# Hops of a four-layer graph network in blocks of 64 tiles, with the scalar chain in two independent halves

## The reference

```python
head_emb = entity_emb[head]; tail_emb = entity_emb[tail]
rel_emb = relation_emb[relation_type]
ricci = _l2_normalize(tail_emb + rel_emb)
hyper_head = expmap0(head_emb)                 # tanh(n) * u / n
hyper_tail = expmap(tail_emb, hyper_head)      # mobius_add(p, tanh(...) * u / n)
hyper_rel = expmap(rel_emb, hyper_head)
res = project(mobius_add(hyper_tail, hyper_rel))
res = jax.nn.relu(logmap(res, hyper_head) + ricci * 1e-07)
sums = zeros.at[head].add(res)                 # then / clip(counts, 1)
...
for _ in range(2):
    e = _l2_normalize(_agg(e, relation_emb, head, tail, relation_type))
    entity_res_emb = 0.5 * entity_res_emb + e
```

## Time and profile before

| | |
|---|---|
| median of three runs | 23802.61 us |
| profiled execution | 24039.33 us |
| its span, mean granted TensorE clock | 24037.5 us, 0.618 |
| DVE busy | 16546.3 us, 69% |
| POOL busy | 12605.7 us, 52% |
| PE busy, weight loads | 10326.4 us, 43%; 6860.3 us, 29% |
| ACT busy | 2139.0 us, 9% |
| hop 0, hop 1 in the span | 16471 to 20166, 20277 to 23976 us |
| DVE busy in each | 2929.34 us, 2935.75 us |

### The profile page before, as it was taken

One profiled execution on the slowest core, in us unless ns is written; L12 is line 12 of the kernel. 1 busy time (PEld: TensorE's weight loads), 2 busy tenths in 40 slices (PEclk: granted clock), 3 DMA queues, 4 the chain that ended last, 5 costly groups with the idle time before them and its releaser, 6 DMA issues. The chain is left out here.

```text
span 24037.5 us, 205919 instructions
## 1 busy us (share of the span) xinstructions
PE 10326.4 (43%) x47565; PEld 6860.3 (29%) x47566; DVE 16546.3 (69%) x26071; ACT 2139.0 (9%) x3670; POOL 12605.7 (52%) x12782
## 2 busy tenths in 40 slices
PE   0033326655555555556666422222333333333333
PEld 0033322222222222222222322222333332333332
DVE  8744439988888888886666211115888886878887
ACT  0011110000000000000000000001111111111111
POOL 0188876655566555536665166653444443444443
PEclk9999997555555555558887555555555555555555
DMA  4133331111111111121112001113111112111112
GB/s 170 25 69 69 69 64 25 24 23 23 22 21 23 23 23 23 22 20 24 24 24 23 9 21 21 21 21 49 52 51 50 51 50 41 52 51 50 52 50 42
DMA packets 1118452, 942.42 MB, mean 39 GB/s; under 512 B 775931, under 2 KB 887579, under 8 KB 1117875
## 3 DMA queue, kind: packets, MB, share of 16 engines
q0 software_dynamic: 419904, 437.84, 9.9%
q1 hardware_dynamic: 698096, 500.67, 8.0%
HBM read 726.46 MB, written 207.32 MB: 39 GB/s over the span
## 5 line engine op out<-in xcount | busy, mean ns | idle before, releaser
L1420 POOL DMA_INDIRECT tail<-ball,h_idx x3328 | 3271.7, 983 | 1793.3 <-issue 1231.1
L736 PE MATMUL p_rad<-w_stack,hid_t 99*128 99x512 bf16 (+1 forms) x6656 | 3079.6, 620 | 2391.3 <-DVEq L826 1161.0
L808 DVE TENSOR_REDUCE red<-prod 128x96 f32<-128x1536 f32 x1664 | 2898.3, 1742 | 3.5
L1098 POOL DMA_INDIRECT l_xg<-h_tab,l_idx x1664 | 1571.2, 944 | 1444.1 <-issue 828.3
L1452 PE MATMUL h_sum<-head,h_hot 128*128 128x64 f32 x6656 | 1444.2, 421 | 1987.4 <-ACT head L1498 1987.4
L1438 PE MATMUL h_head<-ball_parts,hot_t 128*128 x9984 | 1067.6, 281 | 2813.4 <-issue 1578.1
L337 POOL DMA_INDIRECT rec_a<-rec,slot x1600 | 1990.4, 1244 | 517.2 <-issue 500.5
L692 POOL DMA_INDIRECT rec_b<-l_rcb x1600 | 1920.0, 1200 | 571.6 <-issue 570.5
L930 POOL DMA_INDIRECT l_xg<-x_tab,l_idx x1664 | 1571.6, 944 | 1141.8 <-issue 874.0
L946 PE MATMUL l_sum<-outer,l_hot 128*128 128x512 f32 x3328 | 1693.3, 673 | 945.6 <-DVEq L991 869.7
L736 PEld LDWEIGHTS p_rad<-w_stack,hid_t 99*128 99x128 bf16 (+1 forms) x6656 | 774.5, 132 | 4337.7 <-issue 4336.0
(11 more groups left out here) (369 smaller groups left out, 18896.7 us busy)
## 6 DMA issues: line engine op xcount, KB each, us to landing
hot_t<-rows_l SPq DMA_DIRECT2D x208, 512.0 KB
rec_a<-fill SPq DMA_DIRECT2D x128, 728.0 KB, 19.6
l_rec<-rec_a SPq DMA_DIRECT2D x104, 896.0 KB, 4.8
rhot_t<-rows_r SPq DMA_DIRECT2D x208, 384.0 KB
tail<-ball,h_idx POOLq DMA_INDIRECT x3328
t<-in_type SPq DMA_DIRECT2D x100, 500.0 KB
l_xg<-in_x,l_idx POOLq DMA_INDIRECT x1664
l_xg<-x_tab,l_idx POOLq DMA_INDIRECT x1664
```

Source lines behind the costliest of these rows:

```text
L736: ins = pe.matmul(p_rad[j % 2][:, h * 512:(h + 1) * 512], hid_t[j // 4 % 2][0:K3 + 3 * (1 - i), j % 4, i, :], w_stack[i][0:K3 + 3 * (1 - i ...
L808: ch.step(dve.tensor_reduce(red[:, j, :], prod[j % 3][:, :, :], AX, ALU.add))
L1420: pool.indirect_dma_start(tg[q][:, j, :], None, table[:, :], bass.IndirectOffsetOnAxis(ap=idx[q][:, j:j + 1], axis=0)).then_inc(gathered[q ...
```

## The change

A block is HU = 4 units, 64 tiles, 26 blocks per hop. `op` issues each operation of the chain twice, for tiles 0 to 31 and 32 to 63, and each waits only for the last but one. Heads (`hg`), relations (`rg`), `tr` and PSUM's relation buffer have one copy instead of two; tails keep two. The hot matrices are made in half units (8 tiles) in two buffers, behind the products of each unit, and wait for the sums that last used the buffer. PE sums first, then picks b+1; its relation matmuls wait for the copies of the quad before. ACT does its four functions, four relus, then 16 quads in a row. POOL reads indices that SP loads per block from DRAM, waits after gathers 13, 26, 39, 52 and 64, and is let go unit by unit. DVE's compares of b+1 stand in the waits for tanh (two units) and behind the adds (two units); tails and heads of b+1 come last. The diff, cut:

```diff
+HU = 4
@@ hop_phase
-        W, Q, H = 2 * BT, BT // 2, BT // 4
+        W, Q, H, N2 = HU * BT, HU * BT // 4, BT // 4, HU * BT // 2
-        hot = sb("h_hot" + tag, [P, W, P])
+        hot = [sb(f"h_hot{k}" + tag, [P, HP8, P]) for k in range(2)]
-        hg = [sb(f"head{q}" + tag, [P, W, T_PICK]) for q in range(2)]
-        rg = [sb(f"rel{q}" + tag, [P, W, D + 2]) for q in range(2)]
+        hg = sb("head" + tag, [P, W, T_PICK])
+        rg = sb("rel" + tag, [P, W, D + 2])
-        p_rel = [ps(f"h_rel{k}" + tag, [P, 4, P]) for k in range(2)]
+        p_rel = ps("h_rel" + tag, [P, 4, P])
@@ sync
+            def body(b, q, it, left):
+                rows(b, 0)
+                rows(b, 1)
+                if left:
+                    hold(sp, turn, tails_read, b + 1)
+                    lists(b + 1, 1 - q)
+                    hold(sp, turn, ends_used, b + 1)
+                    edge_ends(b + 1, 1 - q)
+                rows(b, 2)
+                rows(b, 3)
@@ gpsimd
-                    hold(pool, turn, tails_used, b + 1)
-                    ch.do(pool.tensor_copy(idx[q][:, :], g["dst_b"][:, bass.ds(b * W, W)]))
+                    hold(pool, turn, idx_in[q], it * 16 + 16)
                     for j in range(W):
+                        if j % BT == 0:
+                            hold(pool, turn, tails_used, b * HU + (j // BT + 1))
...
-                        if j % 8 == 7:
+                        if j % 13 == 12 or j == W - 1:
                             hold(pool, turn, gathered[q], it * (16 * W) + 16 * (j + 1))
@@ tensor
+                    hold(pe, turn, taken, b * Q + (k + 2))
                     for j in range(4):
-                            ins = pe.matmul(p_rel[k % 2][:, j, 0:D + 2], rhot_t[h][:, 4 * i + j, :], rel_parts[:, :], start=True, stop=True)
+                        ins = pe.matmul(p_rel[:, j, 0:D + 2], rhot_t[u % 2][:, 4 * i + j, :], rel_parts[:, :], start=True, stop=True)
...
             def body(b, q, it, left):
-                if left:
-                    pick(b + 1)
                 hold(pe, turn, added, b + 1)
...
+                if left:
+                    pick(b + 1)
@@ vector
+            def hots(q, b, m):
+                z = slice(m * HP8, m * HP8 + HP8)
+                if m >= 2:
+                    dve.wait_ge(sum_done, b * (2 * HU) + (m - 1))
...
                 def op(f):
-                    z = slice(0, W)
+                    for half in range(2):
+                        z = slice(half * (W // 2), (half + 1) * (W // 2))
...
-                    ch.sync()
-                    ch.step(f(S, S2, E, B2, z))
+                        if ch.n > 1:
+                            dve.wait_ge(chain_s, ch.n - 1)
+                        ch.step(f(S, S2, E, B2, z))
...
-                hots(q, b, 0)
+                if left:
+                    compares(b + 1, 0)
+                    compares(b + 1, 1)
                 dve.wait_ge(told, b * 4 + 1)
...
-                hots(q, b, 1)
+                if left:
+                    relation_hots(1 - q, it + q)
                 dve.wait_ge(told, b * 4 + 2)
...
+                for u in range(HU):
+                    z = unit(u)
                     for vec, c in ((h, 16), (t, 18), (r, 19)):
                         ch.step(tt(vec[:, z, 0:D], vec[:, z, 0:D], bc(sc[:, c, z].unsqueeze(2), big), MUL_))
+                    load_chunks()
                     ch.sync()
-                    ch.do(tt(h[:, z, 0:D], h[:, z, 0:D], t[:, z, 0:D], ADD))
+                    ch.step(tt(h[:, z, 0:D], h[:, z, 0:D], t[:, z, 0:D], ADD))
+                    load_chunks()
+                    ch.sync()
+                    dve.sem_inc(tails_used, 1)
                     ch.do(tt(h[:, z, 0:D], h[:, z, 0:D], r[:, z, 0:D], ADD))
                     dve.sem_inc(asked, 1)
+                    for m in range(2):
+                        hots(q, b, 2 * u + m)
+                dve.sem_inc(ends_used, 1)
+                for u in range(HU):
+                    dve.wait_ge(sum_done, b * (2 * HU) + (2 * u + 2))
+                    add_groups(dve, ch, chunk[u * BG:u * BG + BG], acc, lambda k: p_sum[:, u * BG + k:u * BG + k + 1, :])
+                dve.sem_inc(added, 1)
                 if left:
+                    compares(b + 1, 2)
+                    tails(1 - q, it + q)
+                    compares(b + 1, 3)
+                    heads(1 - q, b + 1)
```

More of the change, by code:

```diff
@@ new lines, in quads @@
+            def quads(b):
+                for k in range(Q):
+                    hold(act, turn, picked, b * Q + (k + 1 + AHEAD))
+                    act.activation(hg[:, 4 * k:4 * k + 4, :], p_head[k % 2][:, :, 0:T_PICK], ACT.Copy).then_inc(copied, 1)
+                    act.activation(rg[:, 4 * k:4 * k + 4, :], p_rel[:, :, 0:D + 2], ACT.Copy).then_inc(copied, 1)
+                    act.wait_ge(copied, 2)
+                    act.sem_clear(copied)
+                    act.sem_inc(taken, 1)
@@ L1500, in _ @@
             act.activation(p_row[:, 0:P], g["row"][:, :], ACT.Copy).then_inc(row_ready, 1)
             act.sem_inc(taken, SEED)
-            for k in range(Q):
-                quad(0, 0, k)
+            quads(0)
             all_blocks(act, NW, body)
@@ new lines, in with_relation, with tails, heads @@
+            def with_relation(vec, out, u):
+                ch.do(tt(v2[:, :, 0:NREL3], vec[:, unit(u), T_REL:T_REL + NREL3], rhot[:, unit(u), :], MUL_))
+                ch.do(dve.tensor_reduce(out[:, unit(u)], v2[:, :, 0:NREL3], AX, ADD))
+            def tails(q, it):
+                dve.wait_ge(gathered[q], it * (16 * W) + 16 * W)
+                for u in range(HU):
+                    with_relation(tg[q], tr, u)
+                dve.sem_inc(tails_read, 1)
+            def heads(q, b):
+                t = tg[q]
+                for u in range(HU):
+                    z = unit(u)
+                    dve.wait_ge(taken, b * Q + ((u + 1) * H + SEED))
+                    with_relation(hg, sc[:, HV + 1, :], u)
+                    ch.do(tt(v2[:, :, :], hg[:, z, 0:D], t[:, z, 0:D], MUL_))
+                    ch.do(dve.tensor_reduce(sc[:, HV, z], v2[:, :, :], AX, ADD))
@@ L1700, in body, with load_chunks @@
                 big = [P, BT, D]
-                for half in range(2):
-                    z = slice(half * BT, half * BT + BT)
+                chunk = []
+                def load_chunks():
+                    chunk.extend(chunks(dve, g["map"][1], b * (N2 // PACK) + len(chunk) // PACK))
+                for u in range(HU):
+                    z = unit(u)
                     for vec, c in ((h, 16), (t, 18), (r, 19)):
                         ch.step(tt(vec[:, z, 0:D], vec[:, z, 0:D], bc(sc[:, c, z].unsqueeze(2), big), MUL_))
+                    load_chunks()
@@ L1715, in body @@
-                if left:
-                    tails(1 - q, b + 1, it + q)
-                    heads(1 - q, b + 1, load_chunks)
-                else:
-                    for _ in range(2 * BG // PACK):
-                        load_chunks()
-                if left == 2:
-                    compares(b + 2)
-                for half in range(2):
-                    dve.wait_ge(sum_done, b * 2 + (half + 1 + SEED))
-                    add_groups(dve, ch, chunk[half * BG:half * BG + BG], acc,
-                               lambda k: p_sum[:, half * BG + k:half * BG + k + 1, :])
+                    for m in range(2):
+                        hots(q, b, 2 * u + m)
```

308 lines of the change are left out of this document (152 added, 156 removed).

## The result

| | before | changed |
|---|---|---|
| median, same chip, 4 runs each | 23807.93 us | 24648.76 us |
| lowest and highest | 23789.5 to 23815.58 | 24635.6 to 24695.21 |
| ratio, 95% interval | | 1.0358, 1.034 to 1.0376 |
| profiled execution, its span | 24039.33, 24037.5 us | 24695.21, 24693.1 us |
| period of 64 tiles, median | 2 x 69.0 us | 156.6 us |

The account below looks back on a forecast made before the run. DVE's instruction list was taken to bound each hop. Prologue 118, 25 blocks of 126 and a last 81 gave 3,349 us, 350 less per hop; with +40 outside, -660: median 23,150 us, range 22,850 to 25,100.

Parts of the forecast that it names:

- The chain: DVE's 94 dependent steps, issued for two overlapping halves: 28.1 us per 64 tiles, saving 21.5 us.
- Rival 2: In DVE's chain the steps don't overlap: the 21.5 us come back, period 148 us, 24,250 us; chance 0.06.
- Up to the last sum: Block's path through chain and waits, 36.2 us, then products, last relu and sums, 40.5 us.
- X: Picks of 16 quads after the sums, PE and ACT alternating: eight pairs of 5.6 us, 45 us per block.
- 81 + X: Period of a 64-tile block: 81 us for chain, products, sums and last unit's heads, plus the picks; 126 us.
- floor of 40: Least time for a block's picks of 16 quads: 5.0 us a pair, 40 us.
- rival 1: Picks' signals from PE come late while POOL gathers: picks 83 us, period 164 us, 25,050 us; chance 0.33.
- The second argument: Against late picks: the prologue did 8 quads in 28 us under gathers, giving only 56 us for sixteen.
- 143.2: Time in us the kernel before was taken to need for 64 tiles, two blocks of 71.6 us.
- Outside the hops: Kept features go through DRAM: an extra load, stores and loads of the running sum, +40 us.
- Gathers every 13: POOL waits every 13 gathers instead of 8, saving pauses nobody waits for: nothing, except if picks' signals are late.

Follow-up runs that it names:

- experiment 2: Changed kernel with each chain step waiting for the step in front, still two halves of 32 tiles: 23842.84 us, 1.0121 of the kernel before, quiet chip.
- experiment 7: Changed kernel with the chain in one stream over all 64 tiles, each step waiting for the one in front: 22892.0 us, 0.9724 of the kernel before.
- experiment 5: The changed kernel unedited, on another chip, where PE's signals were not late: 22745.48 us against 23549.26 for the kernel before, ratio 0.9658.
- experiment 10: Kernel before with only its chain split into two streams of 16 tiles, on a chip with late signals: 24375.84 us, 1.0227 of the kernel before.
- experiment 12: Changed kernel with gathers held until the picks of the block before are done, late-signal chip: 23466.14 us, 0.9845 of the kernel before.
- experiment 11: Changed kernel with POOL waiting after every 8 gathers instead of 13, late-signal chip: 23885.59 us against 23829.39 for the kernel before, ratio 1.0019.

## Why the prediction was wrong

**The chain.** Right. Its pairs stand in the profile as worked out:

```profile
22257.13 0.35 DVE L1647 TENSOR_TENSOR sc<-sc 128x64 f32<-128x64 f32 x2
22257.41 0.31 DVE L1648 TENSOR_TENSOR sc<-sc 128x32 f32<-128x32 f32 x2
```

Two steps of 0.18 to 0.23 us end within 0.31 to 0.35. Start to products is 34.2 us; the terms were 34.6 (28.1 + 3.1 + 2.4 + 1.0). Undone, it costs the 21 us (experiment 2). What the prediction left out is that the wider block does most of it: one stream over 64 tiles keeps 18 of the 21 us (experiment 7). So the saving is right, and the overlap that it was put down to carries about 3 us of it. Rival 2 is refuted. The section of the Trainium skill that the prediction sets against the split, "The DRAIN you can't avoid" in VectorE: DVE Perf Modes, also says that a next operation that is not held starts earlier, which the prediction left out; the pairs above agree with that.

**Up to the last sum.** Right: 76.7 us forecast, 76.7 measured (77.4 in experiment 5). From the last quad's copy to the next chain 4.3 us were forecast and some 6 measured, so the period is 83 + X and not 81 + X (156.6 less 73.7).

**X without late signals.** 45 us was too much: 35.3 on quiet chips, below the floor of 40 that I gave and that the range was drawn by. A pair of quads takes 4.4 us (35.3 over eight pairs; 4.2 between the copies at 20399.18 and 20403.39 in experiment 5), not 5.6. In the last block of hop 1 of the changed kernel, without gathers, PE stands 1.4 to 1.6 us before a pair's heads where 1.85 were taken for the loads; where the rest of the 1.2 us lay, in the signals or in overlap of loads and copies, was not measured apart.

**The step that failed** is the term X of the sum. It was put at 45 us, with late signals at nothing, and came to 73.7; 38.4 us of that are lateness (73.7 less 35.3), and over the 50 blocks with picks the 28.7 us that X lay above its term are 1,435 us. Behind it stands the weighing of rival 1. "Other signals are not late beside the same gathers, so it could come from the recording" moved its chance to 0.33. Its mechanism was in the trace before, 202 waits at the place that the change puts on the path, and it came: ACT released at the end of groups, DVE idle before compares and heads. Its size was 83 for X and 25,050 us; it was 73.7 and 24,649. The other signals were not safe either: DVE's to itself stretched beside gathers in experiments 10 and 12. The loss is not the profiled execution's alone: the three others took 24,636 to 24,649 us, 0.2% below it. The second argument, 8 quads in 28 us in the prologue, should have been worked out as a price: it says X 56 with groups of 8, and experiment 11 measured 54.9.

**What the forecast did describe** is the other kind of chip: 3.4% faster there, 2.8% forecast. That it comes so near is in part luck, since X was 10 us too long there and the work behind it 2 us too short. The 22,745 us themselves lie below the range's 22,850.

**The block before.** The 71.59 us of the earlier trace rows are a long block; the median is 69.0, and 52 blocks of 71.6 are the hop only because its first 60 us and more, the prologue, were counted as blocks. For 64 tiles the price is 138.0 and not 143.2, so the change begins to lose at X = 55 (138.0 less 83) and not at 62. Experiment 11, with X 54.9 a draw, bears this out. The sum itself goes by the hop's window and does not use the 143.2; the limit of rival 1 does.

**Outside the hops.** +40 us was forecast. From the last sum of hop 0 to the first compare of hop 1 it is 132.5 us against 119.3 before, and from the last sum of hop 1 to the end 72.1 against 64.4: 21 us in both places. The stores in front of hop 0 can't be told apart, since up to there the trace before is itself 141 us longer than the new one.

**Gathers every 13.** The sum put this at "nothing, except under the next rival". On the late kind it costs 763 us (24,649 against 23,886 in experiment 11, on different chips), nearly all of the net loss. On the quiet kind groups of 8 were not run. The rival named the length of the group, the sum did not price the step from 8 to 13.

## What to carry to other kernels

A wait that costs nothing under another engine's work still has a price; before a change takes the cover away, read that price off the trace and put it into the sum, even where its cause is unknown. The gain of this long dependent chain came first from wider steps, and splitting it into streams added little once they were wide: price the two apart. Time a close decision on more than one chip and more than one occasion.

## What the runs showed of the hardware

- The same program ran in 22,745 us on one chip and 24,649 us on another, and the kernel before in 23,549 and 23,808 us, while runs on one chip agree within 0.3%. Each of the seven chips was used on one occasion, so whether the chip or the occasion makes the difference stays open.
- On three of the seven chips, and in the comparison above, signals of PE raised while POOL's indirect gathers were in flight reached ACT and SP late, up to 15.3 us, and two thirds of the copies over 4 us late came when a group had drained. Held gathers took X from 73.7 to 41.6 us, and blocks without gathers in the same trace have 34.4. With plain DMAs of as many rows of the same length no signal was late (X 35.3). Whether it is the indirect form itself, the 1.25 us that POOL takes over each or the scattered rows, and why four chips did not show it, stays open, and so does whether the recording takes part, which was not tried.
- DVE's waits on its own earlier step grew to 1 us beside the same gathers when steps came 0.1 us apart (experiment 10), and its chain took 39.8 instead of 34.2 us beside them (experiment 12).
- Two independent VectorE steps of 0.18 to 0.23 us overlap: they end within 0.31 to 0.35 us, and a wait on the last step but one does not stop it (34.9 us against 55.9 with a wait on the last, experiments 5 and 2).
